# A three-layer transformer kernel: routing the first batch alone, with reductions over partitions on TensorE

## What is computed

```python
x = x + 0.5 * ffn(layernorm(x))
x = x + attention(layernorm(x))      # 16 heads of 128, rope, causal
x = x + 0.5 * ffn(layernorm(x))      # same weights as the first
```

```python
gate_logits = einsum('bsd,ed->bse', x, gate_w)   # 8 logits a token
topw, sel = top_k(gate_logits, 2)
topw = softmax(topw, axis=1)                     # over the 1024 tokens of a batch
base_up, base_gate = xt @ w_up.T, xt @ w_gate.T  # hidden 704
for e in range(8):
    c = sum(where(sf == e, wf, 0.0), axis=1)
    h_e = silu(base_up + lo_up(e)) * (base_gate + lo_gate(e))
    mixed_h += c * h_e
    lora_down += 2.0 * (c * h_e @ down_A[e].T @ down_B[e].T)
out = mixed_h @ w_down.T + lora_down
```

## Time and profile before

| | us |
|---|---|
| median of 3 runs | 1500.58 |
| lowest, highest | 1499.6, 1502.08 |
| the profiled execution, its own time | 1498.31 |
| its span, first to last instruction | 1496.4 |
| mean granted TensorE clock | 0.989 |

### The profile page before, as it was taken

One profiled execution on the slowest core, in us unless ns is written; L12 is line 12 of the kernel. 1 busy time (PEld: TensorE's weight loads), 2 busy tenths in 40 slices (PEclk: granted clock), 3 DMA queues, 4 the chain that ended last, 5 costly groups with the idle time before them and its releaser, 6 DMA issues.

```text
span 1496.4 us, 25603 instructions
## 1 busy us (share of the span) xinstructions
PE 1419.4 (95%) x8912; PEld 1263.1 (84%) x8912; DVE 1056.3 (71%) x2371; ACT 908.0 (61%) x1882; POOL 790.1 (53%) x701
## 2 busy tenths in 40 slices
PE   6899999699999999999999999999999987899998
PEld 4688888589998999899989998999899976688886
DVE  6576766877767777777677767767776776575665
ACT  3544444577767766777777667776776653444433
POOL 4656354356555555555555555555555533655443
PEclk9899999899999999999999999999999999999999
DMA  4000001000000000000000000000000030000000
GB/s 166 1 1 1 1 1 50 22 8 21 3 8 15 8 8 8 15 8 8 15 1 9 22 1 8 22 1 8 8 1 2 1 110 1 0 15 1 15 15 15
DMA packets 11422, 23.40 MB, mean 16 GB/s; under 512 B 928, under 2 KB 5024, under 8 KB 11168
## 3 DMA queue, kind: packets, MB, share of 16 engines
q1 hardware_dynamic: 11296, 21.78, 4.5%
HBM read 19.68 MB, written 2.10 MB: 15 GB/s over the span
## 4 chain that ended last, share of the span: by engine, by line
PE 85%; DVE 9%; issue 3%; ACT 1%; POOL 1%; DMA 0%; DVEq 0%; ACTq 0%; POOLq 0%
PE ps L1316 25%; PE ps L1318 24%; PE ps L1317 24%; PE ps L1659 9%; DVE ps L1255 2%; DVE pT_l L315 1%; DVE mixed L1027 1%; PE ps L1329 1%; DVE hid L1017 1%; DVE stats L877 1%; POOL um_l L315 0%; DVE hid L1004 0%; DVE part_sum L991 0%; DMA x_sb<-x_in 0%; DVE rot L1192 0%
## 5 line engine op out<-in xcount | busy, mean ns | idle before, releaser
L598 POOL TENSOR_SCALAR probs<-probs,inv_sum 128x128 f32<-128x128 f32 (+7 forms) x256 | 216.4, 845 | 380.0 <-DVE inv_sum L1211 379.9
L1255 DVE CUSTOM_DVE_ANT_0 ps<-ps,causal 128x128 f32<-128x128 f32 (+7 forms) x256 | 195.0, 762 | 211.4 <-PE ps L1318 209.6
L832 ACT ACTIVATE probs<-ps,neg_max 128x128 f32<-128x128 f32 (+7 forms) x256 | 189.3, 739 | 79.9 <-DVE neg_max L1255 79.8
L315 POOL TENSOR_TENSOR hid_l<-hid,hid_h 128x512 fp32r<-128x512 f32 x80 | 107.7, 1347 | 182.5 <-ACT hid_h L681 182.5
L315 DVE TENSOR_TENSOR pT_l<-ps,pT_h 128x512 fp32r<-128x512 f32 (+3 forms) x384 | 200.7, 550 | 3.4 <-ACT pT_h L811 3.1
L811 ACT ACTIVATE pT_h<-ps 128x512 fp32r<-128x512 f32 (+3 forms) x384 | 174.4, 491 | 38.3 <-PE ps L1659 35.9
L587 POOL TENSOR_TENSOR rot_sin<-swapped,rope 128x512 f32<-128x512 f32 x128 | 165.8, 1295 | 54.5 <-ACT swapped L788 54.5
L1659 PE MATMUL ps<-ident,probs 128*128 128x128 f32 x1152 | 171.0, 275 | 22.0 <-DVE pT_l L315 19.1
L1318 PE MATMUL ps<-pT_h,v_l 128*128 128x256 f32 (+1 forms) x640 | 179.6, 281 | 0.0
L1317 PE MATMUL ps<-pT_l,v_h 128*128 128x256 f32 (+1 forms) x640 | 179.4, 280 | 0.0
L1316 PE MATMUL ps<-pT_h,v_h 128*128 128x256 f32 (+1 forms) x640 | 178.5, 279 | 0.8 <-DVE oA_l L315 0.8
(11 more groups left out here) (187 smaller groups left out, 4056.2 us busy)
## 6 DMA issues: line engine op xcount, KB each, us to landing
w_raw<-attn_w SPq DMA_DIRECT2D x32, 256.0 KB, 2.7
w_in<-ffn_w SPq DMA_DIRECT2D x12, 576.0 KB, 8.7
x_sb<-x_in SPq DMA_DIRECT2D x4, 512.0 KB, 5.5
...
w_in<-ffn_w SPq DMA_DIRECT2D x2, 264.0 KB, 5.0
...
```

The lines of the kernel that those rows point to most:

```text
L315: return eng.tensor_tensor(dst, src, high.bitcast(F32), ALU.subtract)
L598: pool.tensor_scalar(probs[s % 4][:, 0:n], probs[s % 4][:, 0:n], inv_sum[:, s % 4:s % 4 + 1], 1.0, ALU.mult, ALU.mult).then_inc(probs_read ...
L832: act.activation(probs[t % 4][:, 0:a * n].rearrange("p (a n) -> p a n", a=a), view, ACT.Exp, bias=neg_max[:, t % 4:t % 4 + 1], scale=-1.0, ...
L1255: dve.tensor_tensor_reduce(out=view, in0=view, in1=causal[:, SEQ - a * n:].rearrange("p (a n) -> p a n", a=a), scale=-SCALE, scalar=HUGE, ...
```

## The change

The routing runs per batch. In both stages only batch 0 (chunks 0 and 1) is routed before chunk 0 begins. Batch 1's routing is done within chunk 0 and the first block of chunk 1: turning of chunk 3 in `slot_a` and its logits in `slot_b` of block 0, picks at block 1, maximum at block 4, sums in the tail block, weights at chunk 1. The maxima and sums over partitions go to TensorE: a transpose, a DVE reduction and a product that spreads it, and a product with a matrix of ones. `first_setup` splits the low parts of `UM_UP` and `UM_GATE` on the DVE (new semaphore `um_low_first`), the two others stay on GpSimd. In the second stage the statistics, normalising, turning, logits, routing, first low-rank and first base products are issued at steps 20 to 39 of the last pair. Chunk 2 is normalised in the last two steps, turned after the attention, chunk 3 after it. The loads of x and of the weights are interleaved. `EARLY_SPLITS` is 3 in place of 4. Buffers of the feed-forward stages stand in a new order, so that they can be written while the attention still uses others; `logitsT` and `xn_of` use parts of `spread`.

```diff
-EARLY_SPLITS = 4
+EARLY_SPLITS = 3
...
+STATS_AT = [20, 21, 23, 24, 35, 37, 39]
+AGGREGATE_AT = [21, 24, 37]
+NORM_AT = [(23, 24), (25, 26), (38, 39)]
+TURN_AT, TURNED_LOW_AT = [(25, 25), (27, 29)], [(26, 27), (28, 31)]
+SPLIT_AT = [27, 33, 38]
+LOGITS_AT, TURN_LOGITS_AT = (31, 32), 33
+PICK_AT, PEAK_AT, SHIFT_AT, SUM_AT, WEIGH_AT = 34, 35, 36, 37, 38
+LOW_RANK_AT, BASE_AT, MASK_AT = (35, 36), (37, 39), 39
...
+            load_x(0)
+            load_x(1)
+            load_ffn([0])
+            load_x(2)
+            load_ffn([1])
             load_expand()
+            load_x(3)
+            load_ffn(range(2, SPLITS))
...
-                pool.partition_all_reduce(whole[:, 0, :], part[:, 0, :], P, bass.bass_isa.ReduceOp.max)\
...
+                    if c == 0 and m == 0:
+                        if f == 1:
+                            keep_logits(f, 2)
+                        layer_norm_high(2 * CHUNKS * f + 3, 3, LN_BANKS[f][3])
+                    if c == 0 and m == FULL:
+                        route_exponents(f, 1)
...
+            def route_peak(f, b):
+
+                dve.wait_ge(peak_turned, 2 * f + b + 1)
+                link(dve.tensor_reduce(peak[0:2, b:b + 1], ps[0:2, REDUCE_BANKS[f][b], AT_TURNED:AT_TURNED + P], AX.X, ALU.max),
+                     f, b, 5)
+                link(dve.tensor_scalar(peak_row[0:2, :], ones[0:2, :], peak[0:2, b:b + 1], None, ALU.mult), f, b, ROUTE_PEAK)
...
+            def um_first_low(g, s):
+
+                dve.wait_ge(um_high, 4 * g + s + 1)
+                low(dve, um_l[:, g % 2, s], part_sum[:, s % 2], um_h[:, g % 2, s]).then_inc(um_low_first, 1)
...
+                mask_low_rank(g, UM_UP)
+                mask_low_rank(g, UM_UP_STEP)
+                um_first_low(g, UM_UP)
+                mask_low_rank(g, UM_GATE)
+                mask_low_rank(g, UM_GATE_STEP)
+                um_first_low(g, UM_GATE)
...
+                        for n, at in enumerate(SPLIT_AT):
+                            if t == at + 1:
+                                if n == 2:
+                                    pool.wait_ge(cm_padded, CHUNKS + 1)
+                                split_ffn(1, n)
...
+            def turn_peak(f, b):
+                pe.wait_ge(route_chain, ROUTE_CHAIN * (2 * f + b) + ROUTE_MAX)
+                pe.transpose(ps[0:2, REDUCE_BANKS[f][b], AT_TURNED:AT_TURNED + P], part[:, 0, 2 * b:2 * b + 2], ident[:])\
+                    .then_inc(peak_turned, 1)
+
+            def spread_peak(f, b):
+                pe.wait_ge(route_chain, ROUTE_CHAIN * (2 * f + b) + ROUTE_PEAK)
+                pe.matmul(ps[:, REDUCE_BANKS[f][b], AT_PEAK:AT_PEAK + 2], peak_row[0:2, :], ident[0:2, 0:2], start=True, stop=True)\
+                    .then_inc(peak_spread, 1)
+
+            def add_up(f, b):
+                pe.wait_ge(route_chain, ROUTE_CHAIN * (2 * f + b) + ROUTE_SUMMED)
+                pe.matmul(ps[:, REDUCE_BANKS[f][b], AT_SUM:AT_SUM + 2], ones[:], part[:, 1, 2 * b:2 * b + 2], start=True, stop=True)\
+                    .then_inc(sums_done, 1)
...
+                if c == 0 and m == 0:
+                    if f == 1:
+                        router_logits(f, 2)
+                    pe.wait_ge(um_raw, 4 * g + 4)
+                    layer_norm(2 * CHUNKS * f + 3, xn_of(3, f), LN_BANKS[f][3])
+                if c == 0 and m == 4:
+                    pe.wait_ge(um_raw, 4 * (g + 1) + 4)
+                    turn_peak(f, 1)
+                if c == 1 and m == 0:
+                    add_up(f, 1)
...
+                        if m == 1 and c == 0:
+                            pe.wait_ge(route_chain, ROUTE_CHAIN * (2 * f + 1) + ROUTE_INDEX)
...
+                    layer_norm(0, xn_of(0, f), banks[0])
+                    layer_norm(1, xn_of(1, f), banks[1])
+                    router_logits(f, 0)
+                    router_logits(f, 1)
+                    low_rank_products(0, 0, 0)
+                    turn_logits(f, 0)
+                    low_rank_products(0, 0, 1)
+                    layer_norm(2, xn_of(2, f), banks[2])
+                    turn_peak(f, 0)
+                    first_base(f, 0)
+                    spread_peak(f, 0)
+                    first_base(f, 1)
+                    add_up(f, 0)
+                    turn_mask(0, FIRST_MASK_BANK[f])
+                    first_spreads(f)
+                    router_logits(f, 2)
+                else:
+                    first_spreads(f)
+                    pe.wait_ge(y_added, 8 * PAIRS)
+                    layer_norm(2 * CHUNKS + 2, xn_of(2, f), banks[2])
...
+                    if last:
+                        if t == LOGITS_AT[0]:
+                            pe.wait_ge(exp_done, STEPS * PAIRS - 1)
+                            router_logits(1, 0)
```

547 lines of the change are left out of this document (317 added, 230 removed).

## The result

The changed kernel takes 1491.18 us (median of 4 runs, 1489.62 to 1493.09) against 1501.33 of the kernel before (4 runs beside it, 1499.6 to 1502.42): ratio 0.9942, 95% interval 0.993 to 0.9954. By the ratio, which all comparisons here use, it is 8.7 us faster (6.9 to 10.5); the two medians as they stand are 10.2 apart. The time lies in the forecast range, but the forecast gain was 18.6, about twice the measured one. A second time, against other runs of before, it was 1491.79 and 0.9949 (0.9936 to 0.9961). The profiled execution took 1489.62 with a span of 1487.5, so its span is 8.9 us shorter than the one before.

What follows compares the result with a forecast made beforehand. TensorE, busy for 95% of the span, was taken as the bound, leaving only idle time and slow clock to win. Gains of 6.0 (first stage) and 12.6 (second) sum to 18.6 us: 1482.0 on the median's scale, range 1475 to 1493.

Steps and rivals of the forecast that it cites:

- the first mark of stage 1: First product needing the gate's `um_l`, first feed-forward stage: forecast at 37.3 instead of 46.81, 9.5 us earlier.
- the drain's list of 24.3 us: End of attention, after step 31's scores: TensorE's listed work takes 24.3 us, the router's chain running beside it.
- the table loads: Tail block: ScalarE loads its function table twice more, 1.28 us each; covered by TensorE work, uncovered 2.6.
- the weight loads: Second-stage load needed at step 27 costs nothing; first-stage loads reordered, DVE and ScalarE reach each later than it lands.
- Rival B: DVE and its port shared with GpSimd eat half: collisions in steps 23 to 26 and behind weight splits; 1490.5, chance 0.15.
- the terms between the marks: First stage, gate's first `um_l` product to second hidden block's first product: chunk 3's turning and logits enter, 3.7 becomes 6.0.
- the net of 6.0: First stage's total gain: second mark 7.2 us earlier, less waits later in chunk 0; bounds 3 and 9.
- The last steps of the attention: Steps 20 to 31: added normalisation and splits partly fill DVE idle time; 1.9 delay plus 1.1 collisions, scores 3.1 us later.
- Mask's turn to first mark: Second stage, mask turned at 1248.7, gate's first `um_l` product at 1258.2; DVE is later, 1.3 us of collision included.
- Between the second stage's marks: Gate's first `um_l` product to second hidden block's first product: chunk 2's logits come in too, 4.0 becomes 7.1 us.
- Chunk 0, 1.2 forecast: After the second mark, first stage: small products, wait for the second pick's index step 0.5 and for sums 0.3.
- The allowance of 2.5 for in-order waits: Second stage: 2.5 us taken off the gain for waits of 17 steps of four engines; net 12.6.

Runs made afterwards that it cites:

- e1: Changed kernel with normalisations of chunks 0 and 1 in steps 23 to 26 writing 8 of 256 columns; steps 20 to 31 took 42.29 us, ratio 0.9925.
- e4: Changed kernel with the first batch's maximum and sum over partitions back on GpSimd in the first stage; first mark 41.44, ratio 0.9981.
- e10: Changed kernel with the transposes of chunks 0 and 1 in steps 25, 27 and 29 issued twice; steps 20 to 31 took 44.46 us, ratio 0.994.
- e3: Changed kernel with GpSimd's low split of weight block 2 waiting for normalised chunk 2 instead of the padded mask; mask's turn to first mark 9.56 us, ratio 0.9924.
- e16: Changed kernel with four instead of three weight splits ahead of chunk 0, first stage only; chunk 0 there 63.49 us, first mark 37.69, ratio 0.9953.
- e17: Changed kernel with four weight splits ahead of the second stage, in steps 32, 33 and 35 of the drain; chunk 0 there 63.40 us, ratio 0.9927.
- e12: Changed kernel with batch 1's sum, weights and mask padding moved earlier, from the tail block to chunk 1's start; chunk 0 64.01 and 63.93 us, ratio 0.9929.
- e5_norm_later: Changed kernel with normalisations of chunks 0 and 1 in steps 24 to 27, turns and low parts later; steps 20 to 31 took 47.89 us, ratio 0.9977.

## Why the prediction was right and wrong

**Right.** The reading of where the time lies; the direction; the first mark of stage 1 (37.3 forecast, 36.0 to 38.3 measured with unedited code there); the drain's list of 24.3 us, in which TensorE is the limit and the router's links are hidden; the table loads, the weight loads, the unchanged rest (149.8 against 149.7 us from the first update of x by chunk 0 to the last but one of the second stage). Rival B had 1490.5 and named the collisions; it came nearest in time, and one of its two places (the normalising of chunk 2 beside a weight split) was a full 2 us. Its other place, five us in steps 23 to 26, was not what happened there: e1 leaves about one us of collision, in step 24 (1.48 in place of 0.47). So B named 3 of the us that were lost, and that its total is off by less than 1 is chance.

The first mark was right in part for another reason. The prediction took the chain ahead of it to be 2.1 us shorter because the DVE splits faster and the gate's part doesn't queue. The kernel before had 1.5 to 1.6 us there in which GpSimd stood although its input was ready, behind its reductions. The change takes that away by moving the reductions to TensorE, and the prediction priced their leaving GpSimd at nothing. This is read from the rows and, for the first stage, borne out by e4.

**Wrong, step by step.** Two sums of the first stage don't add up: the terms between the marks (0.7, 1.4, 0.9, 1.4, 0.5, 1.9) make 6.8, close to the 6.7 measured, and not the 6.0 of the forecast, and those of chunk 0 (0.7, 0.5, 0.3) make 1.5, where the net of 6.0 allows 1.2. Added up rightly the forecast would have been 17.5. The rest is steps that failed:

- *The last steps of the attention, 3.1 forecast, 6.6 measured.* The failed step is that idle time of the DVE (5.7 us) can take up new work. It counted the DVE's work for steps 23 to 28 together, and let half of it vanish. In steps 21 to 26 nearly all of it is paid: the DVE's idle time there is its wait for TensorE, which in turn waits for the DVE's next `pT_l`; it is one chain, not slack. And TensorE's turns of chunk 0 weren't in the sum at all, though the diff lists them in step 25; by the rows they are 1.6 us (e10: eight more, 0.4 to 1.2). In steps 26 to 31, with longer tiles, the added work cost 0.4 in all. The runs show that the xn columns are 0.8 of the 6.6 and that the work costs as much or more in other steps; how the rest divides between statistics, GpSimd's `rstd`, turns and half clock is read from the rows.
- *Mask's turn to first mark, 9.5 forecast, 11.6 measured.* The step was right, its collision term was mis-sized: 1.3 forecast, 2.4 measured on the DVE (3.10 in place of 0.73), 2.0 on the path (e3). A stopped instruction can wait for all of the other engine's one, here 2.79 us. The prediction named this place and this cause.
- *Between the second stage's marks, 7.1 forecast, 9.0 measured.* The gate's low-rank product took 1.1 in place of 0.7, in part at half clock, and then TensorE stood 1.34 for chunk 2's `xnT_l`. The DVE waited 1.07 of it for the high part, which ScalarE makes only behind the last `um_h` and the last `spread` of `first_setup`. The sum let the logits follow the gate's product at once, as if chunk 2 were split by then. That part is read from the rows; no run took it out.
- *Chunk 0, 1.2 forecast, 3.5 measured in both stages.* The failed step is that the prediction put "`EARLY_SPLITS` is 3 in place of 4" at nothing: the fourth split inside chunk 0 costs 1.2 (e16, e17). In the first stage that price could not be saved by moving the split to where e16 put it, since there it cost 1.5 at the first mark. The six small operations in front of `dm_part` cost 0.7 (e12). With both gone 1.4 to 1.7 is left over the kernel before, about the small products and waits of the forecast. The allowance of 2.5 for in-order waits covered this in the second stage; the first had none, and there the 2.3 count in full.

**Chance in one profile.** The first mark varies by 2 us with code that is the same, and with one thing: when the first 512-column products reach their distance of 0.23 us. In seven profiles with unedited code there (the first of the changed kernel among them) they do from 15.1 us on, and the mark lies at 36.0 to 36.3; in six others they stand 0.43 apart until 18.4 to 19.6, and it lies at 37.6 to 38.3. (In e5_norm_later they started 0.6 later than elsewhere, at full rate at once: 36.8.) The kernel before is of the late kind (19.9). The stretch from 14.40 to 18.90 in the first profile of the changed kernel (17 products):

```profile
14.40:18.90 4.50, 4.16 (x17) 3.16 (x18) 3.47 (x13) 1.72 (x3) 2.20 (x4) 1.00 0.91 367
```

and in the repeated one (10 products):

```profile
14.40:18.90 4.50, 4.12 (x10) 3.25 (x11) 3.50 (x13) 1.48 (x3) 2.21 (x4) 1.00 0.91 368
```

The granted clock of the row says 1.00 in both, so here the distance of the products tells more than the column. Of the 10.6 us of the first mark in the first profile some 2 are of this kind; by the repeated one the second mark of stage 1 is 5.5 us earlier, not 7.6. The total of 8.7 is that of the ratio, over all executions.
